# Float16 parts for the q and k projections, and a new timetable for the jobs between score steps, in a one-core attention and feed-forward kernel

## The reference

```python
def reference(x, Wq, Wk, Wv, Wo, weight, alpha, bias):
    h = layernorm(x)
    q = rope(h @ Wq)                 # 16 heads of 16
    k = rope(h @ Wk); v = h @ Wv     # 4 key heads, each shared by 4 query heads
    p = softmax(q k^T / sqrt(256))   # per head, 1024 x 1024
    x = x + layernorm((p v) @ Wo)
    w = ternary(weight) * alpha      # entries -1, 0, 1 by a threshold
    return x + layernorm(layernorm(x) @ w^T + bias)
```

## Time and profile before

| what | value |
|---|---|
| time, median of 3 runs | 1544.87 us (1544.76 to 1545.48) |
| profiled execution: time / span from first to last instruction | 1542.89 / 1540.9 us |
| TensorE matmuls, busy | 1453.7 us (94%) |
| VectorE busy | 1360.0 us (88%) |
| ScalarE busy | 1246.7 us (81%) |
| GpSimd busy | 686.8 us (45%) |
| mean granted TensorE clock | 0.979 |

### The profile page before, as it was taken

How to read it: one execution, slowest core, us unless ns; L and a number is a source line. 1 busy time by engine, 2 the same in 40 slices (tenths; PEclk the granted TensorE clock), 3 DMA queues, 4 the chain that set the end, 5 groups by cost and what they waited for, 6 DMA issues and landing times.

```text
span 1540.9 us, 31812 instructions
## 1 busy us (share of the span) xinstructions
PE 1453.7 (94%) x12182; PEld 481.2 (31%) x12182; DVE 1360.0 (88%) x1565; ACT 1246.7 (81%) x2454; POOL 686.8 (45%) x1115
## 2 busy tenths in 40 slices
PE   6789999999999999999999999999999999999997
PEld 5122322323232332323223232323323232222236
DVE  5788999898989999899998989899998989999924
ACT  2078888888988888888888889888888888989881
POOL 4214074544636355453735446363554535333240
PEclk9589999999999999999999999999999999999999
DMA  3411111312031121312112120301212120220101
GB/s 106 116 26 56 62 28 61 81 46 69 27 101 27 60 57 44 94 33 74 26 61 81 47 69 27 104 24 60 57 46 65 33 78 22 61 50 17 40 16 52
DMA packets 72919, 84.89 MB, mean 55 GB/s; under 512 B 17632, under 2 KB 58464, under 8 KB 71328
## 3 DMA queue, kind: packets, MB, share of 16 engines
q1 hardware_dynamic: 71952, 82.08, 18.8%
q10 hardware_dynamic: 816, 0.79, 0.2%
HBM read 46.66 MB, written 24.64 MB: 46 GB/s over the span
## 4 chain that ended last, share of the span: by engine, by line
PE 46%; DVE 38%; POOL 7%; ACT 4%; issue 3%; DMA 1%; SPq 0%; POOLq 0%; DVEq 0%; ACTq 0%
DVE row_max L1161 31%; PE smax L933 16%; PE pv L955 14%; PE ring L1053 4%; PE ring L1026 4%; ACT probs L835 3%; PE ring L1061 2%; PE ring L1041 2%; PE ring L979 2%; POOL act L423 2%; POOL res L503 2%; DVE sy_bn L1141 1%; PE ring L1003 1%; DVE max_parts L1179 1%; POOL sa_rs L398 1%
## 5 line engine op out<-in xcount | busy, mean ns | idle before, releaser
L1161 DVE TENSOR_REDUCE row_max<-smax 128x1 f32<-128x1024 f32 x1024 | 1206.2, 1215 | 108.5 <-PE smax L933 105.7
L835 ACT ACTIVATE probs<-ring 128x512 f32<-128x512 f32 x2048 | 1104.6, 597 | 167.2 <-PE ring L979 153.3
L933 PE MATMUL smax<-k_rows,q_rows 48*128 48x512 f16 x2048 | 629.4, 389 | 50.3 <-DVE row_max L1161 40.3
L979 PE MATMUL ring<-q_rows,k_rows 50*128 50x512 f16 x2048 | 634.2, 383 | 0.5 <-ACT probs L835 0.2
L955 PE MATMUL pv<-probs,v_cols 128*32 128x256 f32 (+1 forms) x6240 | 603.5, 459 | 4.1 <-ACT heads L889 3.7
L933 PEld LDWEIGHTS smax<-k_rows,q_rows 48*128 48x128 f16 x2048 | 116.7, 94 | 550.7 <-DVE row_max L1161 291.0
L955 PEld LDWEIGHTS pv<-probs,v_cols 128*32 128x32 f32 x6240 | 123.2, 108 | 307.3 <-issue 163.2
L979 PEld LDWEIGHTS ring<-q_rows,k_rows 50*128 50x128 f16 x2048 | 132.2, 93 | 45.1 <-ACT probs L835 39.8
L535 POOL TENSOR_TENSOR attnT<-pairs,inv_rows 128x512 f32<-128x512 f32 x31 | 39.4, 1271 | 235.3 <-DMA inv_rows<-inv_sums_dram 235.3
L514 POOL TENSOR_TENSOR act<-act,bias_sb 128x256 f32<-128x256 f32 x60 | 42.3, 727 | 80.1 <-ACT act L878 80.1
L1026 PE MATMUL ring<-xT,wq_sb 128*128 128x256 f32 x256 | 71.9, 407 | 5.1 <-ACT rot_in L820 5.1
(11 more groups left out here) (155 smaller groups left out, 1099.0 us busy)
## 6 DMA issues: line engine op xcount, KB each, us to landing
q_stage_dram<-q_parts SPq DMA_DIRECT2D x45, 256.0 KB, 2.5
q_rows<-q_stage_dram SPq DMA_DIRECT2D x30, 384.0 KB, 7.8
x_in<-in_L_attn_x SPq DMA_DIRECT2D x8, 1024.0 KB, 6.1
pairs<-heads SPq DMA_DIRECT2D x64, 128.0 KB
inv_rows<-inv_sums_dram SPq DMA_DIRECT2D x32, 256.0 KB
res<-in_L_attn_x SPq DMA_DIRECT2D x16, 512.0 KB, 5.6
out<-res SPq DMA_DIRECT2D x15, 512.0 KB, 3.2
k_rows<-k_stage_dram SPq DMA_DIRECT2D x64, 96.0 KB, 3.3
```

The lines of the kernel that those rows point to most:

```text
L835: eng.activation(probs[:, s % PSLOTS, j, :], ring[:, n % RING, :], ACT.Exp, scale=score_unit).then_inc(ring_read, 1)
L933: mm = eng.matmul(smax[:, side, c, :], q_rows[at:to, qc, kv * KVP + jp, qt * P:(qt + 1) * P], k_rows[at:to, kv, c * 512:(c + 1) * 512], st ...
L979: eng.matmul(ring[:, n % RING, :], k_rows[at:to, g, kt * P:(kt + 1) * P], q_rows[at:to, h.qc, g * KVP + j // 2, :], start=True, stop=True)\
L1161: eng.tensor_reduce(row_max[:, g % 2, at:at + 1], smax[:, side, :, :].rearrange("p c n -> p (c n)"), AX.X, ALU.max).then_inc(max_read, 1)
```

## The change

- The normalised, transposed x is scaled by 1024 as ScalarE copies it, and GpSimd makes two float16 parts of it, x_parts (split_x, four pieces, at steps 1 to 4, or 13 in the first half of its kind). The weights of q and k are scaled by 64 and split once (split_weights). Every Q and K job after the first batch is then three float16 products of parts over 512 columns, in one job where two jobs of 256 columns were; ScalarE's copies undo the scales.
- Q jobs stand at steps 16 and 30 in place of 4 to 7, K in one job at step 6 in place of 14 and 15. The rotation of q is always at step 8 of the following half, staging at step 14, loading at step 16 (were 30 and 6 of the next).
- Both transposes HT stand in step 20. The first float16 part of act is made by GpSimd.
- Statistics of x come two to a step (0 to 3), those of y all at step 16, the last two of the feed-forward at step 30. The y statistics wait for their tile one by one.
- The first split of the maxima is a scalar_tensor_tensor with a tile of zeros in place of a tensor_scalar. K's swap is at step 18 (was 17). The order of K and Q in the counts of semaphores is K, Q0, Q1 throughout.

```diff
+PRODUCTS = ((0, 0), (0, 1), (1, 0))
-PRO_FIRST = {11: [("XT", 0, 0), ("XT", 1, 0)], 12: [("XT", 0, 1), ("XT", 1, 1)], 14: [("K", 0)], 15: [("K", 1)],
+PRO_ALONE = {11: [("XT", 0, 0), ("XT", 1, 0)], 12: [("XT", 0, 1), ("XT", 1, 1)], 14: [("K", 0)], 15: [("K", 1)],
              17: [("Q", 0, 0, 0)], 18: [("Q", 0, 0, 1)], 19: [("Q", 0, 1, 0)], 20: [("Q", 0, 1, 1)]}
+PRO_EARLY = {11: [("XT", 0, 0), ("XT", 1, 0)], 12: [("XT", 0, 1), ("XT", 1, 1)], 17: [("K",)],
+             19: [("Q", 0, 0)], 21: [("Q", 0, 1)]}
 PRO = {0: [("XT", 0, 0)], 1: [("XT", 1, 0)], 2: [("XT", 0, 1)], 3: [("XT", 1, 1)],
-       4: [("Q", 0, 0, 0)], 5: [("Q", 0, 0, 1)], 6: [("Q", 0, 1, 0)], 7: [("Q", 0, 1, 1)],
-       14: [("K", 0)], 15: [("K", 1)]}
+       6: [("K",)], 16: [("Q", 0, 0)], 30: [("Q", 0, 1)]}
 PRO1 = {0: [("V", 0)], 1: [("V", 1)], 2: [("V", 2)], 3: [("V", 3)],
-        4: [("Q", 1, 0, 0)], 5: [("Q", 1, 0, 1)], 6: [("Q", 1, 1, 0)], 7: [("Q", 1, 1, 1)]}
+        16: [("Q", 1, 0)], 30: [("Q", 1, 1)]}
 EPI = {8: [("WO", 0, 1)], 9: [("WO", 1, 1)], 10: [("WO", 2, 1)], 11: [("WO", 3, 1)],
-       20: [("HT", 0)], 22: [("HT", 1)], 25: [("FF", 0, 2)], 27: [("FF", 2, 2)]}
+       20: [("HT", 0), ("HT", 1)], 25: [("FF", 0, 2)], 27: [("FF", 2, 2)]}
-X_MOM_FIRST, X_MOM = (0, 1, 2, 5, 6, 7, 8, 8), (0, 1, 2, 3, 4, 5, 6, 7)
-A_MOM, Y_MOM, F_MOM = (9, 10, 11, 12), (15, 15, 16, 16), (27, 27, 29, 30)
+X_MOM_FIRST, X_MOM = (0, 1, 2, 5, 6, 7, 8, 8), (0, 0, 1, 1, 2, 2, 3, 3)
+A_MOM, Y_MOM, F_MOM = (9, 10, 11, 12), (16, 16, 16, 16), (27, 27, 30, 30)
-ACT_SPLIT, BIAS = {21: 0, 23: 1}, {26: (0, 1), 28: (2, 3)}
+ACT_SPLIT, BIAS = {21: 0, 22: 1}, {26: (0, 1), 28: (2, 3)}
-K_SWAP = 17
+K_SWAP = 18
-Q0_STAGE, Q1_STAGE, Q_LOAD = 30, 30, 6
+Q_STAGE, Q_LOAD, Q_LOAD_FIRST = 14, 16, 6
+X_SPLIT_FIRST, X_SPLIT = {13: (0, 1, 2, 3)}, {1: (0,), 2: (1,), 3: (2,), 4: (3,)}
+        def split_x(eng, h, n):
+            dt, c = XT_JOBS[n]
+            src = xT[:, dt, c * HALF:(c + 1) * HALF]
+            hi, lo = (x_parts[:, m, dt, c * HALF:(c + 1) * HALF] for m in range(2))
+            before = (h.pro - 1) * len(XT_JOBS) + n
+            eng.wait_ge(ring_read, h.done("XT", dt, c))
+            eng.wait_ge(ring_full, h.base)
+            eng.tensor_copy(hi, src).then_inc(x_high, 1)
+            eng.wait_ge(x_high, before + 1)
+            eng.tensor_tensor(lo, src, hi, ALU.subtract).then_inc(x_parted, 1)
+            if h.rot is not None and s == Q_ROT:
+                rotate_q(eng, h, *h.rot)
+                split_q(eng, *h.rot)
+                    if h.rot is not None and s == Q_STAGE:
+                        stage_q(*h.rot)
+                    if h.rot is not None and s == Q_LOAD:
+                        load_q(*h.rot)
+                    elif kind == "Q":
+                        eng.wait_ge(w_parted, 2)
+                        eng.wait_ge(x_parted, (h.pro1 if a[0] else h.pro) * len(XT_JOBS))
+                        at = a[0] * HALF
+                        for k, (xm, wm) in enumerate(PRODUCTS):
+                            for dt in range(DT):
+                                mm = eng.matmul(dst[:, :], wq_parts[:, wm, dt, a[1], :], x_parts[:, xm, dt, at:at + HALF],
+                                                start=(k + dt == 0), stop=(k == len(PRODUCTS) - 1 and dt == DT - 1))
-                eng.tensor_scalar(m1, rows, 1.0 / ROW_UNIT, None, ALU.mult).then_inc(max_split, 1)
+                eng.scalar_tensor_tensor(m1, rows, 1.0 / ROW_UNIT, zeros[:, :, :], ALU.mult, ALU.add).then_inc(max_split, 1)
-                        if s in ACT_SPLIT:
-                            dt = ACT_SPLIT[s]
-                            eng.wait_ge(ring_read, h.done("HT", dt))
-                            eng.tensor_copy(act_parts[:, 0, dt, :], actT[:, dt, :]).then_inc(act_part, 1)
...
```

More of the change, by code:

```diff
@@ L114 @@
 SPLIT_ALL = sum(SPLIT_OPS)
-def turn_of(row, what):
-    return (("K", "Q0", "Q1") if row <= 1 else ("Q0", "K", "Q1")).index(what)
 def rot_at(row, what):
-    return row * ROT_ALL + sum(6 if w else 3 for w in ((0, 1, 1) if row <= 1 else (1, 0, 1))[:turn_of(row, what)])
+    return row * ROT_ALL + {"K": 0, "Q0": 3, "Q1": 9}[what]
 def split_at(row, what):
-    return row * SPLIT_ALL + 2 * turn_of(row, what)
+    return row * SPLIT_ALL + {"K": 0, "Q0": 2, "Q1": 4}[what]
 JOIN_OPS = 8
@@ L134 @@
 ACT_UNIT = 1024.0
+X_UNIT = 1024.0
+W_UNIT = 64.0
 class Half:
     def __init__(self, b, qc, scores=True, maxima=STEPS, turned=range(1, HKV + 1), pro=None, pro1=None,
-                 epi=None, late=None, base=0, first=0, steps=STEPS, load_x=None, mom=None, flush=True,
+                 epi=None, late=None, rot=None, base=0, first=0, steps=STEPS, load_x=None, mom=None, flush=True,
                  after=()):
@@ L185, in jobs @@
         if self.pro is not None:
-            out += (PRO_FIRST if self.early else PRO).get(s, [])
+            out += (PRO_ALONE if self.alone else PRO_EARLY if self.early else PRO).get(s, [])
         if self.pro1 is not None:
@@ L636, in swap_k @@
             def swap_k(h):
-                eng.wait_ge(ring_read, h.done("K", 1))
+                eng.wait_ge(ring_read, h.done("K", 1) if h.alone else h.done("K"))
                 for tile in range(4):
@@ L763, in _ @@
             eng.memset(m_half[:, :], -0.5).then_inc(consts, 1)
+            eng.memset(zeros[:, :, :], 0.0).then_inc(consts, 1)
             eng.memset(k_rows[:, :, :], -ROW_UNIT).then_inc(consts, 1)
@@ L817, in stage_first_q, with move, columns @@
                                   q_parts[:, part, :, 0, :]).then_inc(q_staged[0], 16)
-            def move(dst, src):
-                eng.activation(dst, src, ACT.Copy).then_inc(ring_read, 1)
+            def move(dst, src, unit=1.0):
+                eng.activation(dst, src, ACT.Copy, scale=unit).then_inc(ring_read, 1)
+            def columns(part):
+                return (part[0] * HALF // 2, (part[0] + 1) * HALF // 2) if part else (0, HALF)
             def half(h):
@@ L1011, in projections @@
                             eng.matmul(smax[:, 0, 1, 0:1], ones[:, :], abs_sum[:, :], start=True, stop=True).then_inc(w_prep, 1)
[L1013 to L1014 removed]
+                        if h.alone:
+                            eng.wait_ge(ring_read, h.done("XT", 1, 1))
+                            products = [(wk_sb[:, dt, :, :, :].rearrange("p e i h -> p e (i h)"), xT[:, dt, :])
+                                        for dt in range(DT)]
+                        else:
+                            eng.wait_ge(w_parted, 2)
+                            eng.wait_ge(x_parted, h.pro * len(XT_JOBS))
+                            products = [(wk_parts[:, wm, dt, :, :], x_parts[:, xm, dt, :])
+                                        for xm, wm in PRODUCTS for dt in range(DT)]
+                        first, last = (a[0] * HALF // 2, (a[0] + 1) * HALF // 2) if a else (0, HALF)
+                        for k, (w, xs) in enumerate(products):
                             for half_of, eo in ((0, 0), (0, 1), (1, 0), (1, 1)):
                                 tile = (half_of * 2 + eo) * NPAIR * HKV
[L1017 to L1021 removed]
+                                mm = eng.matmul(dst[tile:tile + NPAIR * HKV, 0:last - first], w[:, eo, :],
+                                                xs[:, half_of * HALF + first:half_of * HALF + last],
+                                                start=(k == 0), stop=(k == len(products) - 1),
                                                 skip_group_check=True)
[L1023 removed]
+                    elif kind == "Q" and h.alone:
                         at = a[0] * HALF + a[2] * HALF // 2
@@ L1235, in half @@
                         if now := due(s, Y_MOM):
-                            eng.wait_ge(y_added, nth_epi * ST + sum(now))
                             if now[0] == 0:
                                 eng.wait_ge(y_norm, RAISED + nth_epi * (ST + 1))
-                            moments(res, st_y, y_mom, *now)
+                            for t in range(now[0], sum(now)):
+                                eng.wait_ge(y_added, nth_epi * ST + t + 1)
+                                moments(res, st_y, y_mom, t, 1)
                             if h.alone and sum(now) == ST:
```

86 lines of the change are left out of this document (49 added, 37 removed).

## The result

The changed kernel takes 1549.57 us, median of 12 runs (1543.89 to 1557.08), beside 1544.9 for the kernel before, measured in the same series. The ratio is 1.0029 (95% interval 1.0017 to 1.0042): slower by 0.3%, where 1514.9 and a gain of 2% were forecast. The profiled execution is one of the longest (1557.08 us, span 1554.8), so I count its stretches against the forecast span of 1510.9 (1540.9 less 30); it is 7.5 us above the median, and the median run has less of what follows.

What follows compares the result with a forecast made beforehand. VectorE sets plain steps, TensorE those with Q jobs, coupled by two PSUM sides. Six A halves at 2.3 us, seven B halves at 2.0, plus 1.6 and 0.4, save about 30 from 1544.87: 1514.9, range 1505 to 1531.

Steps and rivals of the forecast that it cites:

- item 3: Step 8: the output projection waits for attnT, +0.65 us (0.4 to 1.0) in a B half, no stall in an A half.
- Item 1: Q jobs out of steps 4 to 7: saves 3.16 us in a B half, 1.95 in an A half with K.
- Rival (a): More comes back: no lock (-3), step 8 stall covered as loads stop crowding the DMA queue (-4.5): 1507; chance 0.17.
- Item 4: Q job at step 16 beside all y statistics costs 0.2 us; steps 14 to 17: B half +0.1, A half -0.6.
- Item 5: Q job at step 30: steps 30 and 31 +0.54 us, next step 0 gets back 0.18, together +0.35.
- Item 6: Both transposes in step 20: steps 20 to 24 go from 12.8 to 12.85 us in B halves, -0.6 in A halves.
- Item 7: GpSimd's added work stays hidden, with 2.9 us to spare before K's job, 1.3 at step 25, 0.7 at step 20.
- rival (b): GpSimd becomes late: transposes or feed-forward wait 1 us in each of 14 halves, 1529 us; chance 0.17.
- Item 8: VectorE's maxima splits in step 4 held by GpSimd's subtractions: 0.5 us per A half, from 0 to 2 x 1.16.
- Item 9: First A half -1.6 us, late halves -0.4, splitting the weights nothing, the zeros memset 0.1 at most.
- Item 10: SP's queue, staging at step 14 and loading at 16: q_rows land about in time for step 20, cost taken as 0.
- rival (c): Slower: TensorE waits at step 20 for late q_rows, 1558 us if the load takes 12.5; chance 0.07.

Runs made afterwards that it cites:

- experiment 6: The kernel of experiment 5 with the Q and K jobs computed in float32 as before, the splits still made but unread: 1531.78 us.
- experiment 9: The kernel of experiment 1 with the V jobs of B halves at steps 4 to 7 instead of 0 to 3: 1531.24 us.
- experiment 7: The kernel of experiment 5 with the first split of the maxima as a tensor_scalar again: 1514.52 us.
- Experiment 5: The changed kernel with x's transposes, V and x's statistics at steps 4 to 7, K at 14, x's load at 9, k's rotation at 23: 1514.79 us.
- experiment 1: The changed kernel with the 1 MB load of x moved from step 5 to step 9: 1534.55 us.
- experiment 3: The changed kernel with ten dummy matmuls (the fill) ahead of each of step 8's two waits, maxima rows in A halves, attnT in B halves: 1555.66 us.

## Why the prediction was wrong, point by point

The step that failed is item 3, the wait at step 8: it was priced at 0.65 us in B halves and at nothing in A halves, and measured 29.8 in all where 4.55 was forecast. The excess of the profiled execution over the forecast span is 1554.8 - 1510.9 = 43.9 us (that of the median run is 34.7): 29.8 - 4.55 = 25.2 in steps 8 and 9 of thirteen halves, 10 in the rest of these halves (a B half without its wait is 87.6 where 86.65 was forecast, an A half 88.7 where 87.9 was), 5 in the opening, some 4 in the late half and the end.

- **What bounds it.** Right that the engines are coupled and that a job costs only what its partner doesn't hide; experiments 6 and 9 show both sides. Wrong in scope: I looked for what TensorE and VectorE do in the steps that shrink, not for what arrives behind them.
- **Item 1.** Right: steps 4 to 7 are 9.58 in a B half (9.40) and 10.37 in an A half (10.6).
- **Item 2.** Right: a Q job takes 1.40 where 1.42 was forecast.
- **Item 3, the step that failed.** The late half's chain was taken over as it stood, and only attnT was asked about. In B halves that came out in halves 9, 11 and 13 (0.40, 0.45, 0.36); the size came out at the lower end, or under it. In halves 3, 5 and 7 the store landed in 3.3 to 3.5 us instead of 1.45, and the second thing that step 8 needs, the maxima rows, stood behind it in SP's queue. A step 8 that begins at 12.57, as in before, would have hidden both (in half 3 the rows landed at 11.40 and attnT was ready at 12.55). In A halves, "K fills the time, no stall" left out the same rows, though SP's order and their landing could be read in before: 0.15 to 0.40 us of cover against 2.2 us taken from in front of it. And no term had the granted clock falling behind a stall, which made steps 8 and 9 of an A half 1.7 or 3.4 us longer (9.77 and 11.47 against 7.91 to 8.10).
- **Rival (a)** held that the loads no longer crowd the queue at step 8. The opposite is so: q_rows' load went, the load of x stayed, and step 8 came nearer to its landing.
- **Item 4.** Steps 16 and 17 of a B half are 6.37, where 6.05 to 6.1 was forecast: 0.3 too low. In an A half, too, so that it saves 0.3 in steps 14 to 17, not 0.6.
- **Item 5.** Steps 30 and 31 are 5.89 for 5.71, and the next B half's step 0 rose from 3.30 to 3.65 where I had it fall to 3.12: ScalarE, behind after the Q job, sets its start. The term should have been about 1 there, and 0.6 ahead of an A half.
- **Item 6.** B halves were better than forecast (12.56 for 12.85). In A halves I had two transposes hide the lock "even if it stays". One held split is hidden but for 0.25, as half 6 shows; in five of six halves two are held, and 1.19 stays.
- **Item 7.** Right: nothing waits for GpSimd at steps 6, 20 and 25 of these halves, and rival (b) didn't come. A slip in its sum, 12.1 + 2.26 x 2 + 0.5 being 17.1 and the spare 2.5, changes nothing.
- **Item 8.** The 0.5 was put at step 4, where the splits took 0.27 and 0.52 and cost no more than that; the lock that costs time is at step 20, where one more split is held than in before. The second split had the two-tensor form all along; in before it began 0.01 us ahead of GpSimd's next instruction (675.66 against 675.67) and took 0.17, in after it begins 0.11 behind one (505.19 against 505.08) and takes 1.20. The Trainium skill ("SBUF — State Buffer", "Who interferes with whom") says that a VectorE instruction with two SBUF inputs contends with a GpSimd instruction that reads SBUF, and that the later one blocks fully. The trace agrees: 1.18 and 1.20 where 0.17 is usual. The old form was held as well, 1.13 at step 20 of six halves in before, so exchanging the forms frees nothing either way; experiment 7 shows it for the time. The error was in pricing one instruction and one place.
- **Item 9.** The first A half gained nothing: 92.49 here, 90.76 in experiment 7, against 90.80. The three jobs at 17, 19 and 21, with step 20 between them, take steps 17 to 21 to 16.6 (14.8 before), which eats the 1.7 saved at 14 and 15; step 20 alone is 3.69 where a job's step was 3.13, with splits of 0.90 and 1.20 in it. The further 1.7 of this execution is half clock in step 3, 3.96 for 2.21 before. The end, from the start of half 15 on, is 3.4 longer than forecast, among it a projection of 5.39 us where before has 3.71 and a store that landed in 2.6 where before has 1.45.
- **Item 10 and rival (c).** Right to take 0: no matmul of step 20 waits for q_rows, and the load lands in 5.6, median of the page, less than before (7.8).

```profile
q_rows<-q_stage_dram SPq DMA_DIRECT2D x30, 384.0 KB, 5.6
```

Experiment 5 ends at the forecast time, 1514.8 for 1514.9. That is no confirmation: its timetable is another one, and the misses of items 4 to 6 are made up by steps 0 to 3.

Left open: the stall at step 8 of the two late halves (3.4 to 4.2 for that step in every version but the fill), which no version covers; how a transfer of instructions delays a store, and whether the store alone, moved in SP's queue, would free the B halves, which no run tried; and the rotation at step 23 in the kernel before, which wasn't tried.

## What to carry to other kernels

When work is taken out from in front of a point, list everything that the point needs, with the time at which each arrives now, transfers too; what arrives a little before its reader shows in no list of waits and may be the next bound. Read the issuing queue in order: here a small transfer behind a large one, behind one that waited for a buffer, or behind a wait for an earlier store, was as late as that one. Price a stall of TensorE with the spell of half clock that may follow it (1.7 or 3.4 us here), and put extra work of two coupled engines into the same steps.

## What the runs showed of the hardware

- Two 4 KB transfers behind a 1 MB load from the same engine's queue landed 5.66 us after the second was issued; with the load behind them (experiment 1, the same half) it was 2.5. The Trainium skill ("DMA: Bandwidth & Descriptors", "Queues, rings and completion order") says that a transfer's completion is written only after all earlier writes of the same DMA engine, whichever queue they came from. The trace agrees in kind: the rows landed at 466.96, the load at 467.14.
- Of eight halves with a long stall in one profiled execution, the five in which TensorE idled 1.54 to 2.13 us in step 8 went on at a granted clock of one half for 3.4 or 6.8 us; the three with 1.26 to 1.45 did not. An idle time of 1.67 in experiment 3, with dummy matmuls close behind it, had no spell.
- A 16 KB store landed in 1.41 to 1.47 us wherever no transfer of instructions ran beside it (304 in twelve traces) and in up to 3.5 us where one did; all 49 over 1.5 us had one.
- A VectorE instruction of 16 elements per partition took 1.18 to 1.27 us beside a GpSimd multiply, in its two-tensor form, and 1.13 beside a multiply or 0.83 beside a subtraction in its one-tensor form, against 0.17.
